# Last cross-attention: the turned scores follow three slots behind the plain ones instead of four

## The reference, cut to what matters

```
def _L3_xattn_ref(values, keys, queries, Wv, Wk, Wq, Wo, bo):
    v = (values @ Wv.T).reshape(N, -1, H, D)
    k = (keys @ Wk.T).reshape(N, -1, H, D)
    q = (queries @ Wq.T).reshape(N, -1, H, D)
    energy = jnp.einsum('nqhd,nkhd->nhqk', q, k)
    attn = jax.nn.softmax(energy / jnp.sqrt(jnp.float32(E)), axis=3)
    out = jnp.einsum('nhql,nlhd->nqhd', attn, v).reshape(N, -1, H * D)
    return out @ Wo.T + bo
...
x = _layernorm(x + _L3_xattn_ref(ctx_1024, ctx_1024, x, ...), axis=-1)
```

## Time and profile before

| | |
|---|---|
| median of 3 runs | 2771.44 us (2770.93 to 2774.01) |
| the profiled execution's own time | 2771.96 us |
| its span in the trace | 2770.1 us |
| busy, share of the span | PE 87%, DVE 58%, ACT 45%, POOL 37% |
| stage l3_xattn | 2335.7 to 2536.0 us of the span |
| of it: loading before the first score | to 2357.5 us |
| filling slots 0 to 3 | 2357.5 to 2402.2 us |
| mixed slots 4 to 15 | 2402.2 to 2495.4 us |
| tail slots 16 to 19 | 2495.4 to 2526.5 us |
| last values, last output and normalization | to 2536.0 us |

### The profile page before, as it was taken

How to read it: one execution, slowest core, us unless ns; L and a number is a source line. 1 busy time by engine, 2 the same in 40 slices (tenths; PEclk the granted TensorE clock), 3 DMA queues, 4 the chain that set the end, 5 groups by cost and what they waited for, 6 DMA issues and landing times. The chain is left out here.

```text
span 2770.1 us, 46327 instructions
## 1 busy us (share of the span) xinstructions
PE 2399.0 (87%) x16011; PEld 1416.2 (51%) x16011; DVE 1595.0 (58%) x3815; ACT 1233.6 (45%) x3220; POOL 1037.3 (37%) x901
## 2 busy tenths in 40 slices
PE   4979998599679999998999989999597995996998
PEld 2446666255435555555555555556355443454443
DVE  3544544375367777877777777776364223573233
ACT  1324451155246665666666666666152111263121
POOL 2010000101178777877777777776101002000000
PEclk8989999798789999999999999999797897797999
DMA  2100000100010000000000000000000010000010
GB/s 60 24 26 1 1 1 1 15 3 2 13 39 5 20 14 12 16 17 13 13 16 25 9 10 24 9 9 1 8 10 4 27 30 12 12 2 24 23 34 19
DMA packets 42848, 41.97 MB, mean 15 GB/s; under 512 B 6973, under 2 KB 31717, under 8 KB 42612
## 3 DMA queue, kind: packets, MB, share of 16 engines
q1 hardware_dynamic: 42612, 38.95, 5.4%
HBM read 33.36 MB, written 0.52 MB: 12 GB/s over the span
## 5 line engine op out<-in xcount | busy, mean ns | idle before, releaser
L3286 POOL TENSOR_TENSOR l1fb_p<-l1fb_p,l1fb_rden 128x640 f32<-128x640 f32 x192 | 240.8, 1254 | 258.6 <-DVE l1fb_rden L3353 258.6
L3278 POOL TENSOR_TENSOR l1fb_rinv<-l1fb_ssq,neghalf 128x8 f32<-128x8 f32 x192 | 315.4, 1643 | 8.8 <-DVE l1fb_ssq L3343 8.7
L3482 PE MATMUL ps<-l1fb_wqkv,l1fb_xs 128*128 128x512 f32 x576 | 298.0, 627 | 9.0 <-DVE l1fb_xs L3309 4.3
L3438 ACT ACTIVATE l1fb_p<-ps,l1fb_shift 128x128 f32<-128x128 f32 (+1 forms) x768 | 282.7, 393 | 0.3
L3348 DVE TENSOR_REDUCE l1fb_shift<-ps 128x4 f32<-128x640 f32 x192 | 157.8, 822 | 107.1 <-PE ps L3512 105.5
L3280 POOL TENSOR_TENSOR l1fb_qk<-l1fb_qk,l1fb_rinv 128x512 f32<-128x512 f32 x192 | 202.6, 1055 | 15.1
L3419 ACT ACTIVATE l1fb_sq<-ps 128x512 f32<-128x512 f32 x192 | 114.9, 599 | 173.5 <-PE ps L3482 163.0
L3438 ACT ACTIVATION_READ_ACCUMULATOR l1fb_p<-ps,l1fb_shift 128x1 f32 x768 | 169.0, 220 | 0.0
L3498 PE MATMUL ps<-ident,l1fb_qk 128*128 128x128 f32 x768 | 126.8, 288 | 37.4 <-DVE l1fb_attT L3362 28.8
L3512 PE MATMUL ps<-l1fb_kT,l1fb_qT 64*128 64x128 f32 (+1 forms) x1536 | 147.6, 311 | 0.0
L3336 DVE TENSOR_TENSOR l1fb_r<-ps,l1fb_turn_tab 128x256 f32<-128x256 f32 x384 | 142.8, 413 | 0.0
(11 more groups left out here) (708 smaller groups left out, 5362.0 us busy)
## 6 DMA issues: line engine op xcount, KB each, us to landing
l1fb_wqkv<-in_L_ffn_Wqkv SPq DMA_DIRECT2D x24, 256.0 KB, 2.7
l3f_w<-in_L_ffn_W SPq DMA_DIRECT2D x21, 256.0 KB, 3.1
l2f_w<-in_L_ffn_W SPq DMA_DIRECT2D x16, 256.0 KB, 3.1
l1fb_wqkv<-in_L_ffn_Wqkv SPq DMA_DIRECT2D x6, 512.0 KB, 3.9
l1fb_wo<-in_L_ffn_Wo SPq DMA_DIRECT2D x6, 512.0 KB, 4.2
l1fb_w<-in_L_ffn_W SPq DMA_DIRECT2D x6, 341.0 KB, 2.9
l3x_k<-l3x_k SPq DMA_DIRECT2D x8, 128.0 KB
l1fb_w<-in_L_ffn_W SPq DMA_DIRECT2D x6, 128.0 KB
```

The lines of the kernel that those rows point to most:

```text
L3278: nc.gpsimd.tensor_tensor(w.rinv[:, u, :], w.ssq[:, u, :], chip.neghalf[:, 0:8], ALU.pow).then_inc(*w.unit_norm.end(f"rinv{u}"))
L3286: nc.gpsimd.tensor_tensor(p, p, w.rden[:, c, :, :].rearrange("p j q -> p (j q)").unsqueeze(2).to_broadcast([P, 2 * QT, SEEN]), ALU.mult)\
L3438: last = nc.scalar.activation(w.p[:, c % 4, j, q, 0:hi - lo], ps[:, SCORE_BANK(c) + j, lo:hi], ACT.Exp, bias=w.shift[:, c, j, q:q + 1], ac ...
L3482: nc.tensor.matmul(ps[:, PROJ_BANK(u), :], w.xs[:, x.odd, q * P:(q + 1) * P], w.wqkv[:, col:col + 512], start=True, stop=True)\
```

## The change

The distance between plain and turned scores becomes a parameter of `Strips` (`lag`, LAG = 4 unless given), and this stage alone passes 3. With it:

- turned scores run in slots 3 to 18 and values in slots 4 to 19, each a slot sooner; slots 0 to 2 are filling, slots 3 to 15 mixed, slots 16 to 18 tail;
- the identity matmuls (L414 in the profile) run in slots 0 to 2 only;
- the shift of a pair moves from step 3 of its slot to step 1 of the same slot (in the other three attentions it stays in the last step);
- heads move from slot 4b + 2m + 7 to 4b + 2m + 6 (step 0), turn_at goes from 10 to 9, so turn and out run a slot sooner;
- PE's wait for the second half's keys and values moves from the end of slot 3 to the end of slot 2.

```
-    def __init__(self, nc, chip, ctx, label, NH, NK, turn_at=None):
+    def __init__(self, nc, chip, ctx, label, NH, NK, turn_at=None, lag=LAG):
...
-        self.turn_at = turn_at
+        self.turn_at, self.lag = turn_at, lag
...
-                self.misc[b * G + 2 * m + 2, self.last] = ("shift", b, m)
-                self.misc[b * G + 2 * m + 7, 0] = ("heads", b, m)
+                self.misc[b * G + 2 * m + 2, self.last if lag == LAG else 1] = ("shift", b, m)
+                self.misc[b * G + 2 * m + lag + 3, 0] = ("heads", b, m)
...
-            elif slot < LAG:
+            elif slot < h.lag:
...
-                    if h.here(slot - LAG):
-                        scoresT(slot - LAG, u, i, p)
+                    if h.here(slot - h.lag):
+                        scoresT(slot - h.lag, u, i, p)
...
-            if h.here(slot - LAG - 1):
-                values(slot - LAG - 1, u)
+            if h.here(slot - h.lag - 1):
+                values(slot - h.lag - 1, u)
...
-            t = slot - LAG
+            t = slot - h.lag
...
-            t = slot - LAG - 1
+            t = slot - h.lag - 1
...
-        h = Strips(nc, chip, ctx, "l3x", 16, S2, turn_at=16 // STRIPS + 6)
+        h = Strips(nc, chip, ctx, "l3x", 16, S2, turn_at=16 // STRIPS + 5, lag=3)
...
-                if (slot, u) == (LAG - 1, h.last):
+                if (slot, u) == (h.lag - 1, h.last):
                     eng.wait_ge(*act.done("k3"))
                     eng.wait_ge(*dve.done("v3"))
```

More of the change, by code:

```diff
@@ L343, in masks @@
                                  mask[0].rearrange("p t k -> p (t k)"), start=True, stop=False)
-        if h.here(slot - LAG):
+        if h.here(slot - h.lag):
             for i in range(2):
-                scoresT_free(slot - LAG, u, i)
-                nc.tensor.matmul(ps[:, 3 + h.bank(*h.group(slot - LAG), u, i), :], chip.ident_b[:, :], mask[1].rearrange("p t k -> p (t k)"), start=True, stop=False)
+                scoresT_free(slot - h.lag, u, i)
+                nc.tensor.matmul(ps[:, 3 + h.bank(*h.group(slot - h.lag), u, i), :], chip.ident_b[:, :], mask[1].rearrange("p t k -> p (t k)"), start=True, stop=False)
     def scores(t, u, i, p):
```

## The result

Six runs of each give medians of 2760.08 us (2756.43 to 2761.67) after and 2771.18 us (2769.36 to 2774.66) before, a ratio of 0.9957 with an interval of [0.9944, 0.9969]. A second comparison of the same kernel gave 0.9948 [0.9936, 0.9961]. The two intervals span a gain of 8.6 to 17.7 us. The forecast was 2758.5 us, a gain of 12.9 us. The profiled execution took 2759.69 us (span 2757.9) against 2771.96.

What follows compares the result with a forecast made beforehand. Filling steps were taken as bound by a VectorE-PE round trip, the stage as paying by the slot. -13.58 + 0.28 + 0.32 + 0.1 = -12.9 us gave 2758.5 us (chance 0.81), range over all 2755 to 2763.3.

Steps and rivals of the forecast that it cites:

- The stage pays by the slot: Whole attention stage: a slot of turned scores costs nearly the same with plain scores beside it or without.
- Slot 3 becomes mixed: Behind step (2, 3): four low-clock filling steps go, the 8.97 us stretch to the first values slot stays; saves 13.58 us.
- Later slots: The 15 slots that follow: one mixed slot replaces a tail slot, +0.28 us; one shift more, +0.32 us.
- First shift at (2, 1): Filling step: shift copy and values copy slightly exceed VectorE's idle time; cost 0.1 us, bounds 0 and 0.4.
- The margin of the shifts: Shift lands 2.9 us after its transposes start, waiting turned score due at 3.7; margin 0.8 us, cost 0.
- Rival A: First shift stuck behind the second half's key loads, 3 us late, low clock a step longer: 2762 us; chance 0.07.
- Rival B: Clock stays low as long as before, to about 2406.9, through some nine steps: 2763 us; chance 0.06.
- C: Every shift lands late and turned scores wait at slots 3, 5, ... 17: slower, 2777 us; chance 0.03.
- D: No gain: shifts land after about 4 us, waits for them give back the saved slot: 2771 us; chance 0.03.
- The end: Last values, heads, turn, out and normalization move as a whole chain with the last exponentials; no cost.

Runs made afterwards that it cites:

- the pairs in the table: Kernel before and changed kernel, filling altered alike: no identity matmuls, medians 7.9 us apart; doubled, 9.8; 56 matmuls ahead, 12.5; as it is, 11.1 and 14.7.

## Why the prediction was right, point by point

**The stage pays by the slot: right.** One slot fewer, and the pairs in the table show what a slot is worth at each length of its steps.

**Slot 3 becomes mixed: right in mechanism, low by 2.4 us in the profile.** The step that was mis-sized is "I expect that same 8.97 directly behind 2388.85", with the clock falling in slot 2 as before. It did not fall: 1.1 us were won up to (2, 3) (2.23 for 3.31) and 1.3 from there to slot 4 (7.69 for 8.97). Of these 1.3 us the clock accounts for 1.0, two mixed steps of 1.54 in place of 2.05. The other 0.25 is the last step, which took 1.79 before, with a shift at its end, and 1.54 after, without one: the prediction left that shift in the 8.97 and charged it again in slot 4. It gave 0.5 us as its bound on this side and did not consider that the fall itself could go.

Why the fall went, two of the experiments show better than the pair itself. From the clock's rise (2.9 us behind the first maxima in all five kernels) the profiles have:

| distance | first shift at | clock holds for | then |
|---|---|---|---|
| 4 (before, two profiles) | (2, 3) | 23.9 us | falls in the filling |
| 3 (shift in step 3) | (2, 3) | 23.9 us | falls in the filling |
| 4 (shift in step 1) | (2, 1) | 30.7 us | falls in the filling |
| 3 (shift in step 2) | (2, 2) | 27.3 us | falls 0.8 us behind the wait of 1.27 us |
| 3 (the changed kernel, two profiles) | (2, 1) | 153.6 us | falls in the last output of the stage |

The first row's window, from the kernel before, has the same work as that of the kernel with the shift in step 3, shown above:

```profile
2362.50:2386.40 23.90, 20.70 (x120) 11.02 (x120) 13.65 (x22) 4.79 (x4) 0.00 (x0) 1.00 0.23 34
```

At 23.9 us all of them are still in the filling, which in the changed kernel goes on to 25.1. So what took the clock past this point is not the shorter filling but the first shift, two steps earlier: on TensorE, two small transposes and an idle time of 0.25 us in place of 0.46 in that step are all that differs. TensorE at that step, in the changed kernel and in the kernel before:

```profile
2385.00 0.38 PE L392 MATMUL ps<-ident,l3x_nm 128*8 128x128 f32 x2
...
2385.84 0.39 PE L414 MATMUL ps<-ident_b 128*128 128x512 bf16 x1 [0.25 <-DVE l3x_nm L475]
```
```profile
2384.06 0.39 PE L414 MATMUL ps<-ident_b 128*128 128x512 bf16 x1 [0.46 <-DVE l3x_nm L475]
```

The shorter filling did the second part: where distance 4 falls, at 30.7 us, the changed kernel has been in mixed work for 5 us. Why so small a difference moves the fall is open, and three of the rows are single profiles.

**Later slots: right.** Forecast +0.6 (0.28 for the mixed slot, 0.32 for the shift), measured +0.52. Slots with heads and shift took 7.77, forecast 7.7 to 7.8.

**First shift at (2, 1): right.** The step behind it is 2.23, as without it: 0 us for a forecast of 0.1. What the move did to the clock was not foreseen.

**The margin of the shifts: right**, and shown from the other side by the kernel in which it is a step shorter. Rival A did not come: there is no wait for `l3x_shift`. But by the semaphore events in the trace the first shift landed 2.06 us after its issue, where the other seven took 1.67 to 1.71 and the key loads ahead of it ended 1.9 us after its issue; nearly half of the margin was gone there. In stage l1a of the kernel before, whose wait spoke for A, the shift took 6.85 us to land with the key loads still under way. Rival B did not come either, the clock was higher than forecast and not lower. Rivals C and D did not come, but C's price was too small.

**The end: wrong by 1 us.** "A chain that moves as a whole" left out that the clock's fall behind the last values need not move with it. It fell 0.2 us into the last output in both profiles of the changed kernel, and behind it in six others, the two of before among them (18.3 us from the last exponentials to the next stage); in five of the remaining six it fell within the last output, and with the shift in step 3 long before it.

That the median came near the forecast owes something to luck, to errors of opposite sign in the profiled pair: -2.4 in the filling, +1.0 at the end, +2.2 outside the stage, which no theory here explains and which lies within the 5 us that runs of one kernel differ by.

## What to carry to other kernels

When a software pipeline is filled by one chain of round trips and later carries two that overlap, shortening the lead is worth the filling slot at the filling's own step length; measure that length at the clock level it meets, for it may be half as long again there. Before moving a transfer closer to its reader, add up the path (transpose, copy, issue, landing: 2.9 us here) and compare it with the steps left; with 3.7 us left the move was free, with 2.0 it cost about 0.7 us a time, and with 0.3 it cost more than the wait, because TensorE's clock went with it. Work added only to keep the clock up must be paid where the clock is already low: doubling it lengthened slots 0 and 1 by 6.7 us and saved 5.2 from there to slot 5. And when a change moves a small job within a stretch where the clock is about to fall, compare kernels that differ in that job alone before the fall is put down to something else.

## What the runs showed of the hardware

- The clock's course is repeatable to about 0.2 us relative to the kernel's own steps: two profiles of the kernel before fall at (2, 2) to (2, 3), two of the changed kernel nowhere in the filling. Moving a job of two small transposes by two steps moved the fall by 6.8 us (23.9 to 30.7 us behind the rise, distance 4, one profile of the latter).
- A wait of TensorE of 2.2 to 2.6 us amid dense work came with at least 3.4 us at the low level in five of five cases, and 15.3 us of waits became 36 us of time. Of the six shorter waits, five of 0.56 to 0.65 us were followed by no fall, and one of 1.27 us, at the end of the filling, by one of 6.8 us. The Trainium skill, page "TensorE: Matmul & The Clock Gate", section "A second HAM failure mode: psum-queue depth-cycling", says that a TensorE which idles briefly between groups of matmuls swings between its two levels. The filling of the kernel before agrees with it: TensorE idles 0.46 us in its steps of 2.23 us, and the clock falls in the midst of it; that of the changed kernel has the same idle times and shows no fall.
- 12 us of matmuls ahead of the filling kept the clock at its upper level for 41 us on end, but then it fell for 17 us, under the filling that it survives in the changed kernel without them (for 31 us in the kernel before). In both it fell 21 us behind the first maxima; in the kernel before without them, 27 us behind. Keeping the clock up early did not keep it up later.
- A filling step with identity matmuls takes 2.23 us at the high and 3.39 at the low level, a factor of 1.5; one without them 1.5 (1.96 with a copy of values on VectorE) and 2.0.
